# Attention, then a token-shift mix, on one core: the mix's first weights and first chunk prepared inside attention's last group

## The reference

```python
# attention (16 heads of 32), h = layernorm(x)
ct_q  = h @ Wd_q + b;   query = heads(ct_q @ Wu_q + b) + heads(rope(ct_q @ Wq_r + b))
ct_kv = h @ Wd_kv + b;  key   = heads(ct_kv @ Wu_k + b) + heads(rope(h @ Wk_r + b))
value = heads(ct_kv @ Wu_v + b)
x = x + softmax(query @ key^T / sqrt(16 + 256 + 256)) @ value @ Wo + bo
# mix, h = layernorm(x), h_prev = h shifted by one token, zeros first
xr = mu_r * h + (1 - mu_r) * h_prev
xk = mu_k * h + (1 - mu_k) * h_prev
x = x + sigmoid(xr @ W_r^T) * (relu(xk @ W_k^T)^2 @ W_v^T)
```

## Time and profile before

| | us |
|---|---|
| median of 3 runs | 3128.22 (3125.77 to 3131.85) |
| profiled execution | 3131.6, its span 3129.5 |
| PE busy | 3023.1 (97%) |
| DVE / ACT / POOL busy | 2237.4 / 1487.7 / 2093.2 |
| attention's groups end, mix starts | 2307, 2309 |

### The profile page before, as it was taken

How to read it: one execution, slowest core, us unless ns; L and a number is a source line. 1 busy time by engine, 2 the same in 40 slices (tenths; PEclk the granted TensorE clock), 3 DMA queues, 4 the chain that set the end, 5 groups by cost and what they waited for, 6 DMA issues and landing times. The chain is left out here.

```text
span 3129.5 us, 42700 instructions
## 1 busy us (share of the span) xinstructions
PE 3023.1 (97%) x15424; PEld 2010.3 (64%) x15424; DVE 2237.4 (71%) x3346; ACT 1487.7 (48%) x2712; POOL 2093.2 (67%) x715
## 2 busy tenths in 40 slices
PE   8999999989999999999999999999967999999998
PEld 5888888855555555555555555555426777877776
DVE  5555655668777777777777777777528778678784
ACT  2222222136666666666666666666633223223232
POOL 1111221138999999999999999999944665665663
PEclk9999999989999999999999999999978999999999
DMA  4545445564646555565646465555233323313311
GB/s 146 175 168 170 172 168 181 177 154 99 145 104 144 114 131 125 122 137 120 141 104 146 101 147 110 135 123 122 58 119 87 108 67 95 107 55 106 107 54 41
DMA packets 188920, 381.76 MB, mean 122 GB/s; under 512 B 17088, under 2 KB 53088, under 8 KB 180704
## 3 DMA queue, kind: packets, MB, share of 16 engines
q1 hardware_dynamic: 179696, 313.70, 36.4%
q0 software_dynamic: 9072, 66.06, 10.3%
HBM read 194.59 MB, written 118.49 MB: 100 GB/s over the span
## 5 line engine op out<-in xcount | busy, mean ns | idle before, releaser
L355 DVE TENSOR_REDUCE part_max<-ps_m 128x1 f32<-128x512 f32 x1984 | 1214.4, 682 | 334.6 <-PE ps_m L339 333.6
L1006 POOL TENSOR_TENSOR pairs<-probs 128x2048 f32<-128x2048 f32 x255 | 1180.3, 4634 | 145.3 <-ACT probs L979 132.4
L979 ACT ACTIVATE probs<-ps_s 128x512 f32<-128x512 f32 x2048 | 1036.7, 621 | 297.1 <-PE ps_s L871 280.9
L339 PE MATMUL ps_m<-k_stack,q_stack 96*128 96x512 f32 x1984 | 821.4, 415 | 16.3 <-DVE neg_max L352 9.1
L871 PE MATMUL ps_s<-q_stack,k_stack 97*128 97x512 f32 x2048 | 816.6, 402 | 5.7 <-PEq L387 3.7
L339 PEld LDWEIGHTS ps_m<-k_stack,q_stack 96*128 96x128 f32 x1984 | 376.5, 190 | 290.3 <-DVE part_max L355 136.7
L884 PE MATMUL ps_o<-probs,v_tiles 128*32 128x512 f32 x4096 | 497.8, 604 | 0.0
L871 PEld LDWEIGHTS ps_s<-q_stack,k_stack 97*128 97x128 f32 x2048 | 388.7, 190 | 128.3 <-ACT probs L979 20.3
L1013 POOL TENSOR_TENSOR pairs<-pairs 128x2048 f32<-128x2048 f32 x63 | 288.3, 4576 | 4.9
L602 POOL TENSOR_TENSOR ln_rstd<-ln_rstd,ln_minus_half 128x4 f32<-128x4 f32 x15 | 15.1, 1008 | 411.1 <-DVE ln_rstd L644 411.1
L884 PEld LDWEIGHTS ps_o<-probs,v_tiles 128*32 128x32 f32 x4096 | 107.6, 109 | 237.2 <-issue 178.2
(11 more groups left out here) (187 smaller groups left out, 4794.3 us busy)
## 6 DMA issues: line engine op xcount, KB each, us to landing
pairs<-pairs POOLq DMA_DIRECT2D x63, 1024.0 KB, 7.6
q_stack<-q_hi_scratch SPq DMA_DIRECT2D x128, 256.0 KB, 6.3
k_stack<-k_hi_scratch SPq DMA_DIRECT2D x64, 512.0 KB, 10.9
x_in<-in_x SPq DMA_DIRECT2D x16, 1024.0 KB, 5.5
q_hi_scratch<-st_hi SPq DMA_DIRECT2D x64, 256.0 KB, 2.1
q_lo_scratch<-st_lo SPq DMA_DIRECT2D x64, 256.0 KB, 2.4
k_hi_scratch<-st_hi SPq DMA_DIRECT2D x64, 256.0 KB, 2.3
k_lo_scratch<-st_lo SPq DMA_DIRECT2D x64, 256.0 KB, 2.6
```

The costliest lines, as they stand in the source:

```text
L339: nc.tensor.matmul(bank[:, :], att["q"][r][0:ROWS, half, h, q * P:(q + 1) * P], att["k"][r][0:ROWS, h, kc * CH:(kc + 1) * CH], start=True, ...
L355: nc.vector.reduce_max(part_max[:, half, j, kc:kc + 1], bank[:, :], AX).then_inc(att["m_read"], 1)
L979: nc.scalar.activation(probs[:, (r * UNITS + u) % PR, x // HG, x % HG, :], ps_s[place(u * UT + x) % SR][:, :], ACT.Exp, scale=SCALE).then_ ...
L1006: nc.gpsimd.tensor_tensor(pairs[:, w, :, :], probs[:, (r * UNITS + u) % PR, 0, :, :], probs[:, (r * UNITS + u) % PR, 1, :, :], ALU.add).th ...
```

## The change

What it does, part by part:

1. Buffers. The slots are now whole tensors of 128 partitions. Slots 0 and 2 are handed out at addresses that buffers of the mix take over: slot 0 those of o_hi, o_lo, w_o_lo, x_in, bo and one quarter of gate; slot 2 those of w_o_hi, w_k_lo, w_r_lo, w_k_hi and relu. Raw weights are loaded where their low parts will stand, and the inverse of batches 0 to 6 where w_o_hi will stand. The groups 30 and 31 use slots 0 and 1, so slot 2 is free from group 30 on, slot 0 from group 31 on.
2. neg_max has one buffer for both halves; the negation of a half waits for the copy of the half before it.
3. Group 30: SP loads the sums of batches 0 to 6, W_k and W_r raw, mu_r and mu_k. Group 31: SP loads W_o, chunk 0 of o, bo and x, and, after the last stores of group 30, stores the inverse of seven batches and loads chunk 0's inverse.
4. Group 31, ACT: the high parts of W_o (it waits for the inverse's store), W_k and o, ahead of units 3, 4 and 7. DVE: the reciprocal of seven batches, division of chunk 0, low parts of W_o, W_k, o.
5. attend_block no longer waits for its stores at the end. SP waits for them in the mix, before it loads the sums of batch 7.
6. The mix starts with project(0). Chunk 1's inverse goes into ka_hi. POOL's list is add_bias(0), divide(1), inv_std(0), o_low(1), edge(0), add_bias(1). DVE's is: low part of W_r, reciprocal of batch 7, norm(0), low part of W_v, first_shift, first_shift_low.
7. The first token shift is done by quarters of 512 columns, through xT[1] in place of mixed, with ACT making each quarter's high part in between.
8. gate is three quarters and one quarter in two tensors, and each chunk is stored with two DMAs.

```diff
 # max_reduce / stack_max
-        if not is_first(m):
-            dve.wait_ge(att["m_stacked"][half], 16 * m)
-        nc.vector.tensor_scalar(neg_max[:, half, :], bank[0:HALF_TILES, 0:P], -1.0, None,
+        if half == 1 or not is_first(m):
+            dve.wait_ge(att["m_stacked"][1 - half], 16 * (m + half))
+        nc.vector.tensor_scalar(neg_max[:, :], bank[0:HALF_TILES, 0:P], -1.0, None,
 # attend_block, SP
+            def weights_of_the_mix():
+                for q in range(NQ):
+                    sp.wait_ge(l_stored[q], 16 * FC * (B - 1))
+                sp.dma_start(mix["sums"], by_batch(l_s)[:, 0:B - 1, :]).then_inc(mix["l_loaded"], 16)
+                for k, src in (("k", wk_d), ("r", wr_d)):
+                    load_weight(k, src)
...
+            def first_chunk_of_the_mix():
+                load_weight("o", wo_d)
+                for q in range(NQ):
+                    sp.wait_ge(o_stored[q], 16 * FC)
+                load_heads(sp, mix, o_d, 0, 0)
+                sp.dma_start(mix["bo"], bo_d.rearrange("(a n) -> a n", a=1).broadcast_to([P, D])).then_inc(mix["small_loaded"], 16)
+                sp.dma_start(mix["x_in"], x_v[0, 0]).then_inc(mix["x_loaded"], 16)
+            def first_inverse_of_the_mix():
+                sp.wait_ge(mix["inv_done"], 1)
+                sp.dma_start(by_batch(inv_d)[:, 0:B - 1, :], mix["inverse"]).then_inc(mix["inv_stored"], 16)
+                sp.wait_ge(mix["inv_stored"], 16)
+                load_inverse(sp, mix, inv_d, mix["o_lo"], 0, 0)
             def step(i, r, n):
-                if not (type(n) is int and n + 2 >= NG):
-                    if not is_first(n):
-                        sp.wait_ge(pv_done, n * UNITS)
-                        sp.sem_inc(held, 1)
+                if not is_first(n):
+                    sp.wait_ge(pv_done, n * UNITS)
+                if n + 2 < NG:
                     load_group(sp, att, scratch, n + 2, (r + 2) % R3)
+                elif n + 2 == NG:
+                    weights_of_the_mix()
+                else:
+                    first_chunk_of_the_mix()
                 if not is_first(n):
                     store_o(n - 1, 1)
                     store_l(n - 1, 1)
-                if not is_last(n):
+                if is_last(n):
+                    first_inverse_of_the_mix()
+                else:
                     stack_max(sp, held, att, n + 1, (r + 1) % R3, 0)
...
-            for s in o_stored + l_stored:
-                sp.wait_ge(s, 16 * NG)
 # attend_block, ACT
+                    if is_last(n) and u == ROUNDS - 1:
+                        act.wait_ge(mix["inv_stored"], 16)
+                        weight_high("o")
+                    if is_last(n) and u == ROUNDS:
+                        weight_high("k")
+                    if is_last(n) and u == UNITS - 1:
+                        act.wait_ge(mix["o_div"], 1)
+                        nc.scalar.copy(mix["o_hi"], mix["o_in"][:]).then_inc(mix["oh_done"], 1)
 # attend_block, DVE, last group
+                dve.wait_ge(mix["l_loaded"], 16)
+                nc.vector.reciprocal(mix["inverse"], mix["sums"]).then_inc(mix["inv_done"], 1)
+                dve.wait_ge(mix["o_loaded"], 16)
+                dve.wait_ge(mix["inv_loaded"], 16 * HG)
+                nc.vector.tensor_tensor(mix["o_in"][:], mix["o_in"][:], mix["o_lo"].bitcast(F32), ALU.mult).then_inc(mix["o_div"], 1)
+                weight_low("o", 1)
+                weight_low("k", 2)
+                dve.wait_ge(mix["oh_done"], 1)
+                nc.vector.tensor_tensor(mix["o_lo"], mix["o_in"][:], mix["o_hi"], ALU.subtract).then_inc(mix["ol_done"], 1)
 # mix_block, SP
+            load_heads(sp, mix, o_d, 0, 1)
+            load_inverse(sp, mix, inv_d, first_inverse, 0, 1)
+            sp.dma_start(diff[:], wv_d.rearrange("(c p) n -> p c n", p=P)).then_inc(w_loaded["v"], 16)
+            for stored in mix["l_stored"] + mix["o_stored"]:
+                sp.wait_ge(stored, 16 * NG)
+            sp.dma_start(sums, by_batch(l_d)[:, B - 1:B, :]).then_inc(l_loaded, 16)
 # mix_block, ACT
-            weights_high("o")
-            o_high(0)
-            for k in ORDER[1:]:
+            for k in ORDER[2:]:
                 weights_high(k)
+            o_high(1)
             x_T(0, 0, 0)
-            o_high(1)
-            highs(0)
+            first_highs()
 # mix_block, POOL
+            divide(1)
             inv_std(0)
+            o_low(1)
             edge(0)
-            divide(1)
-            o_low(1)
 # mix_block, DVE
+            def first_shift():
+                def low(f):
+                    dve.wait_ge(*((xkh_done, 1) if f == FC - 1 else (first_hi, f + 1)))
+                    nc.vector.tensor_tensor(xk_lo[:, f, :], first_mix[:, f, :], xk_hi[:, f, :],
+                                            ALU.subtract).then_inc(xkl_done if f == FC - 1 else first_lo, 1)
+                dve.wait_ge(zero_done, 1)
+                dve.wait_ge(w_split_lo, len(ORDER))
+                for f in range(FC):
+                    dve.wait_ge(xT_done, f + 1)
+                    cur, prev = xT[0][:, f, 1:CH + 1], xT[0][:, f, 0:CH]
+                    nc.vector.tensor_tensor(diff[:, f, :], cur, prev, ALU.subtract).then_inc(diff_done if f == FC - 1 else first_diff, 1)
+                    dve.wait_ge(*((diff_done, 1) if f == FC - 1 else (first_diff, f + 1)))
+                    nc.vector.scalar_tensor_tensor(first_mix[:, f, :], diff[:, f, :], mu_k[:, f:f + 1], prev,
+                                                   ALU.mult, ALU.add).then_inc(xk_done if f == FC - 1 else first_mixed, 1)
+                    if f >= 1:
+                        low(f - 1)
+                low(FC - 1)
+                for f in range(FC):
+                    v = nc.vector.scalar_tensor_tensor(diff[:, f, :], diff[:, f, :], mu_r[:, f:f + 1], xT[0][:, f, 0:CH],
+                                                       ALU.mult, ALU.add)
+                v.then_inc(xr_done, 1)
...
+            weights_low(2)
+            dve.wait_ge(l_loaded, 32)
+            nc.vector.reciprocal(inv, sums).then_inc(inv_done, 1)
             dve.wait_ge(small_loaded, 16 * 3)
             norm(0, 0)
-            nc.vector.reciprocal(inv[:, 1:B, :], sums[:, 1:B, :]).then_inc(inv_done, 1)
-            shift(0, 0, 0)
-            shift_low(0)
+            weights_low(3)
+            first_shift()
+            first_shift_low()
             chunks(dve, body)
```

More of the change, by code:

```diff
@@ new lines, in raw_weights2, with mix_start @@
+def raw_weights2(sb):
+    return [sb("early_inverse", [P, B - 1, SC]), sb("raw_skip2", [P, FC * D - (B - 1) * SC])] + [sb(f"raw_{k}", [P, FC, D]) for k in "kr"]
+def mix_start(buffers, raw, inverse, own, sem):
+    return {
+        **{k: buffers[k][:] for k in ("o_hi", "o_lo", "x_in", "bo", "gate3", "relu")},
+        "o_in": own("o_in", [P, FC, CH]),
+        "w_hi": {k: buffers[f"w_{k}_hi"][:] for k in "ok"},
+        "w_lo": {k: buffers[f"w_{k}_lo"][:] for k in "okr"},
+        "w_raw": {k: a[:] for k, a in zip("okr", raw)},
+        "sums": buffers["relu"][:].rearrange("p r t -> p (r t)")[:, 0:(B - 1) * SC].rearrange("p (b c) -> p b c", b=B - 1),
+        "inverse": inverse[:],
+        "mu_r": own("mu_r", [P, FC]), "mu_k": own("mu_k", [P, FC]),
+        "w_loaded": {k: sem(f"w_loaded_{k}") for k in "okrv"},
+        "small_loaded": sem("small_loaded"),
+        "x_loaded": sem("mix_x_loaded"), "o_loaded": sem("o_loaded"), "inv_loaded": sem("inv_loaded"),
+        "o_div": sem("o_div"), "oh_done": sem("oh_done"), "ol_done": sem("ol_done"),
+        "w_split_hi": sem("w_split_hi"), "w_split_lo": sem("w_split_lo"),
+        "l_loaded": sem("l_loaded"), "inv_done": sem("inv_done"), "inv_stored": sem("inv_stored"),
+        "o_stored": [sem(f"o_stored{q}") for q in range(NQ)],
+        "l_stored": [sem(f"l_stored{q}") for q in range(NQ)],
+    }
@@ new lines, in by_batch, with load_inverse @@
+def by_batch(a):
+    return a.rearrange("(b h) t -> b (h t)", b=B).rearrange("b (p c) -> p b c", p=P)
+def load_inverse(sp, mix, inv_d, dst, b, par):
+    cs = slice(par * CH, (par + 1) * CH)
+    inv_v = inv_d.rearrange("(b g a) t -> b g a t", g=FC, a=HG)
+    for a in range(HG):
+        sp.dma_start(dst[a * HD:(a + 1) * HD, :, :].bitcast(F32),
+                     inv_v[b, :, a, cs].rearrange("(o g) t -> o g t", o=1).broadcast_to([HD, FC, CH])
+                     ).then_inc(mix["inv_loaded"], 16)
@@ L738, in _, with attend_block @@
             body(last_i, True)
-def attend_block(nc, sem, held, t, att, scratch, o_d, l_d):
+def attend_block(nc, sem, held, t, att, scratch, o_d, l_s, inv_d, slot2, mix, x_v, wo_d, wr_d, wk_d, bo_d, mur_d, muk_d):
     KB = 2
@@ L801, in attend_block @@
         o_out = sem("o_out")
-        o_stored = [sem(f"o_stored{q}") for q in range(NQ)]
-        l_stored = [sem(f"l_stored{q}") for q in range(NQ)]
+        o_stored, l_stored = mix["o_stored"], mix["l_stored"]
         block = ctx.enter_context(nc.Block())
```

(21 more changed lines are left out.)

192 lines of the change are left out of this document (94 added, 98 removed).

## The result

The kernel after takes 3108.43 us (median of 4 runs, 3107.7 to 3112.89), the kernel before on the same chip 3126.99 (4 runs, 3125.06 to 3131.85): ratio 0.9939, 95% interval 0.9924 to 0.9954, 18.6 us less. The forecast was 3109. The two profiled executions lie further apart, 3131.6 and 3107.7, because the one of before was its slowest run and the one of after its fastest.

A forecast was written before the change was run, and what follows sets the result against it. TensorE, busy almost throughout, loses time at the seam between attention and mix. First k product 2384.0 - 2364.1 = 19.9 us earlier, less 0.4 for the second store, 19.5; 3128.2 - 19.5 gives 3109, range 3101 to 3117.

The forecast's parts named there:

- last group longer: Last attention group: ScalarE's added copies and wait for the inverse's store delay it 1.2 us; ends 0 and 10.
- unit 3 / unit 4 late: Last group on ScalarE: unit 3 starts 1.7 us late, unit 4 gives some back, at most 2 late.
- GpSimd's last addition ends before the sums ask: Last group: VectorE's splitting pushes GpSimd's last addition to 2302, barely hidden from PE; at most 2 us if not.
- projection, length: Mix's first projection: at full clock, 0.24 us a matmul, it takes 11.5 us instead of 13.3.
- last sums land: Mix's start: the last batch's sums land 0.6 us after wv's 2322.6; VectorE waits for them before norm(0).
- T, from the mix's start: End of chunk 0's normalisation, held 4.5 us by GpSimd's o_low(1): 2337.5, 28.6 us from the mix's start.
- T to the first k product: From chunk 0's normalisation end through VectorE's first token shift, held 5.2 us by GpSimd's add_bias(1): 24.8 us.
- PE's idle ahead of it: Between project(1)'s end and the first k product PE idles 7.6 us; before it had no gap.
- slow products behind it: After PE's idle the clock falls to 1.2 GHz: nine slow matmuls, 1.8 us.
- first k product, from the mix's start: First k product 53.4 us after the mix's first instruction; outside 48 to 58 would be wrong.
- steady parts: Attention groups and steady mix chunks stay as far apart as before.
- Rival A: Seam: lock falls the other way or transfers land sooner, no 4.5 hold, no 1.8 clock loss; 26 us, 3102; chance 0.20.

The follow-up runs named there:

- the second experiment: Kernel after with GpSimd's low part of chunk 1 (o_low(1)) moved behind edge(0), away from the root's end; one run, 3106.73 us.
- the fourth experiment: Kernel after with VectorE's reciprocal of the last batch, and its wait for the sums, behind norm(0); 3104.79 us (4 runs), ratio to before 0.9929.
- the third experiment: Kernel after with GpSimd's o_low(1) ahead of the reciprocal root instead of behind it; one run, 3107.72 us.
- the fastest kernel: Kernel after with late reciprocal, later weight copies, whole-tensor first shift, and chunk 1 divided and split by VectorE inside norm(0); 3097.99 us, ratio 0.9900.
- the combined one: Kernel after with late last-batch reciprocal, ScalarE's last-group weight copies later, and first token shift by whole tensors; 3104.23 us (4 runs), ratio 0.9923.

## Why the prediction held

| step, as predicted | predicted | in the trace |
|---|---|---|
| last group longer | 1.2 | 2.2 |
| unit 3 / unit 4 late | 1.7 / at most 2 | 3.1 / 3.7 |
| GpSimd's last addition ends before the sums ask | 2302 | 2301.34, no wait |
| projection, length | 11.5 | 11.1 |
| last sums land | 2323.2 | 2324.4 |
| T, from the mix's start | 28.6 | 29.0 |
| T to the first k product | 24.8 | 22.4 |
| PE's idle ahead of it | 7.6 | 7.8 |
| slow products behind it | 1.8 | 2.2 |
| first k product, from the mix's start | 53.4 | 51.4 |
| steady parts | as before | 1.9 shorter |

The units' lateness is against the earlier trace rows less the 1.44 us by which everything ahead of them ran earlier (SyncE's store of l, 2261.31 in the earlier trace rows, 2259.87 here).

The mechanism was as told: the first projection at once and at full clock, the last sums as the wait behind it, then the lock. T came out near because the lock was charged as a whole instruction (4.5; the trace has 6.09 in place of 1.91, so 4.2). That followed and the page "SBUF — State Buffer" of the Trainium skill (Who interferes with whom); by the small delay alone T would have been 24.8 from the start, and the trace has 29.0. That it is as near as 0.4 us is a balance: the last sums came 1.1 later from the mix's start than forecast, the additions and the lock took 0.3 less each. Rival A, the lock falling the other way, was in effect run as the second experiment: it frees T and gives nothing in k, so its 4.5 us were not there to be had that way.

Three terms were off in size, and partly cancelled. The last group: the inverse's store, behind 3.25 MB of loads, landed in 5.8 us and not in the 4.1 that I had worked out (2262.2 to 2266.3), and unit 3 was 3.1 late instead of 1.7. (Of the nine traces with this store seven have 5.8 to 5.9 us and two, those of the second and the fourth experiment, 4.0 and 4.1.) Unit 4 did not win some of that back, as I had it: after the copy of W_k ScalarE still waited 1.92 us for PE, and the unit was 3.7 late. That is the term "1.2 us for the group", measured 2.2, and by the later experiments not a constant. From T to k: I let GpSimd's four additions lock VectorE out for their full 5.2 us on top of 8.5 for the quarters and 0.75 for the last copy, 14.45; the stretch took 12.38 (2340.33 to 2352.71). Four operations in it were held (three of 1.78 in place of 0.68, one of 1.66 in place of 0.75), 4.2 in all, and the lock fell partly into times in which VectorE waited for ScalarE's high parts anyway. mu_r was 2.73, not 3.0. And the steady chunks: not predicted, 1.9, cause not shown.

The clock term was right for a reason that its row does not give. I read "gaps of that length" from 0.50 at 2332, but that stretch follows an idle of PE of 27.33 us, not of 7 to 8. What shows it for this length is the trace of after: 7.84 us of idle, then products 0.43 us apart up to 2365.28.

The sum: predicted 21.7 us to the start of k, less 1.8 for the clock, less 0.4, 19.5. Measured in the profiles 22.0, less 2.2, plus 1.9, plus 0.5 to the end, 22.2; over the medians 18.6. With a spread of 5 to 7 us in the runs of either kernel, and with three errors of size that partly cancel, the agreement to 0.6 is partly luck. So is that of PE's idle time (7.6 and 7.8): k came 2.4 earlier behind T than forecast, but project(1) also ended 2.6 earlier (T + 14.6, not T + 17.2), because I had given it the 13.3 us of a projection with nine slow products and it took 11.2. What is no luck is that the lock holds until the other's instruction has ended: the second and the third experiment show it by moving it.

What I did not see is how much was left: the wait for sums that only the last batch needs (3.6 us by the medians, though the two intervals overlap), and GpSimd's two big operations ahead of and behind the root. The change took 18.6; another 10.4 by the medians (12.9 if each is set against the before beside it) lay in the order of the same instructions and in which engine does them.

## What to carry to other kernels

Where VectorE and GpSimd both have work on a path, price each meeting by the other's whole instruction, not by one's own size, and give the long two-input operation to the faster of the two (here 2.3 us on VectorE, 4.5 on GpSimd) in a place where it would only wait for the other's answer. A load, a reciprocal or a split that only a later chunk needs belongs behind the first chunk's chain. Work put into a stage that is bound elsewhere was nearly free here where it was a load (the group of 58.4 us with all loads in it), and not always where it was an operation: ScalarE's stall and copy made unit 3 3.1 us late, and VectorE's splitting, which pushed GpSimd's additions back, cost nothing in after and 2.35 us of PE's time in another trace. A stall that lets PE idle can cost clock as well.

## What the runs showed of the hardware

- The mutual lock in both directions, with small and large operations: 0.17 us became 2.53 (VectorE, four columns), 0.69 became 4.99, 1.03 became 3.01 (GpSimd, four columns), 2.29 became 6.66. A normalisation piece, which takes one tensor in, was held by GpSimd too (longest 4.72 us), as the row below of all 64 says (min/median/max ns). The reciprocal of 896 columns was not held: 5.73 us at 2246.73 while GpSimd added, 5.75 in before, where GpSimd was idle for all but the last microsecond of it.

```profile
L1525 DVE TENSOR_SCALAR mixed<-xs,mix_mv,mix_rstd x64: 532/538/4722, 2331.9 to 3037.5; 128x512 f32<-128x512 f32 x64
```

- PE's clock in the last attention group is not the same from run to run at an equal list of instructions: over the group it was 0.87 to 0.92 in the five traces with after's list, 0.86 to 0.94 in the three with the copies moved, 0.91, 0.91 and 0.97 in the three with before's. Nothing here says what tips it. The length of the group (59.5 to 63.7 us in the five) does not follow the clock alone.
- PE's idle of 4.7 us ahead of k in the fastest kernel was still followed by a stretch at 0.50 (2353 to 2358); after 3.2 us in the second experiment the first five products came 0.24 us apart or less, but from 2361.15 on they came 0.43 apart, and the stretch from 2359 to 2364 had 0.69.
- Single chunks of the steady mix were 3 to 4 us longer in two profiles (50.6 from store to store in that with the late reciprocal, where PE waited 3.4 for a low part on GpSimd; 51.2 in the combined one); their others were 46.8 to 49.3. A gain of 3 us at the seam can be lost so in one execution.
